# Products of probabilities and values for two head groups back to back, with three sets of transposed probabilities

## What is computed

```python
x = x + mamba(layernorm(x))            # a state-space mixer with a residual of its own
x = x + xattn(layernorm(x), ctx, mask) # 16 heads of 16 features over 512 x 512 scores
x = x + ffn(layernorm(x))              # each position goes through one of 8 matrices

# xattn, for each batch, head and query:
scores = Q @ K.T / 4 + adj; scores[mask == 0] = -inf
out = softmax(scores) @ V              # then the output projection
```

## Time and profile before

| | us |
|---|---|
| median of 3 runs | 1271.53 |
| lowest and highest | 1267.21, 1273.34 |
| the profiled execution: its time | 1269.45 |
| its span, first to last instruction | 1267.7 |

### The profile page before, as it was taken

How to read it: one execution, slowest core, us unless ns; L and a number is a source line. 1 busy time by engine, 2 the same in 40 slices (tenths; PEclk the granted TensorE clock), 3 DMA queues, 4 the chain that set the end, 5 groups by cost and what they waited for, 6 DMA issues and landing times. The chain is left out here.

```text
span 1267.7 us, 29908 instructions
## 1 busy us (share of the span) xinstructions
PE 1141.1 (90%) x10292; PEld 788.5 (62%) x10292; DVE 996.4 (79%) x2530; ACT 782.1 (62%) x1452; POOL 636.1 (50%) x554
## 2 busy tenths in 40 slices
PE   4587999999999999999999999999999999887387
PEld 2255666666667677666766666767776676655244
DVE  5765888788879887888888887888888887755486
ACT  2224675767776677667766766767566776766242
POOL 4572466327833584446544773278144653300375
PEclk9798999999999999999999999999899999989699
DMA  6042105410432024401540053103240143020511
GB/s 206 0 117 76 51 1 146 116 32 26 113 96 85 26 68 105 122 4 42 133 129 16 26 151 99 46 26 103 75 124 2 45 98 96 25 57 19 208 78 58
DMA packets 101524, 96.52 MB, mean 76 GB/s; under 512 B 17184, under 2 KB 76832, under 8 KB 100096
## 3 DMA queue, kind: packets, MB, share of 16 engines
q1 hardware_dynamic: 92912, 76.42, 20.0%
q0 software_dynamic: 6240, 17.57, 5.9%
q10 hardware_dynamic: 2224, 0.62, 0.2%
HBM read 71.49 MB, written 27.26 MB: 78 GB/s over the span
## 5 line engine op out<-in xcount | busy, mean ns | idle before, releaser
L902 ACT ACTIVATE T<-T,nmx 128x512 f32<-128x512 f32 x512 | 368.7, 723 | 215.6 <-DVE nmx L1269 213.6
L1269 DVE CUSTOM_DVE_ANT_0 T<-ps,am 128x512 f32<-128x512 f32 x512 | 346.3, 684 | 117.0 <-PE ps L687 115.2
L695 PE MATMUL pt<-ident,T 128*128 128x128 f32 x2048 | 324.8, 283 | 15.2 <-ACT PT L893 14.4
L695 PEld LDWEIGHTS pt<-ident,T 128*128 128x128 f32 x2048 | 231.9, 142 | 121.0 <-issue 87.8
L893 ACT COPY PT<-pt 128x512 f32<-128x512 f32 x352 | 201.9, 573 | 15.8 <-PE pt L695 15.1
L1385 POOL TENSOR_TENSOR dmask<-triu,dA 128x1024 fp32r<-128x1024 f32 x64 | 132.5, 2134 | 49.7 <-DVE dA L1113 49.5
L687 PE MATMUL ps<-k_st,q_st 64*128 64x512 f32 x512 | 131.0, 504 | 22.1 <-DMA q_st<-q_d 21.6
L712 PE MATMUL po<-PT,va 128*32 128x128 f32 x4096 | 139.2, 277 | 10.4 <-issue 6.2
L1360 POOL TENSOR_TENSOR xc<-xc,ygT 128x512 f32<-128x512 f32 x90 | 119.5, 1328 | 13.4
L1423 POOL TENSOR_TENSOR rr<-se,nhalf 128x1 f32<-128x1 f32 x32 | 22.1, 690 | 207.2 <-DVE se L1199 200.2
L712 PEld LDWEIGHTS po<-PT,va 128*32 128x32 f32 x4096 | 105.4, 110 | 33.3 <-issue 32.1
(11 more groups left out here) (216 smaller groups left out, 1950.3 us busy)
## 6 DMA issues: line engine op xcount, KB each, us to landing
k_st<-k_d SPq DMA_DIRECT2D x256, 64.0 KB, 2.2
q_st<-q_d SPq DMA_DIRECT2D x256, 64.0 KB, 2.4
am<-in_mask SPq DMA_DIRECT2D x8, 1024.0 KB, 5.4
k_d<-kp SPq DMA_DIRECT2D x32, 256.0 KB, 2.7
am<-in_adj POOLq DMA_DIRECT2D x8, 1024.0 KB, 10.6
q_d<-qp SPq DMA_DIRECT2D x128, 64.0 KB, 1.6
x_in<-in_x SPq DMA_DIRECT2D x8, 512.0 KB, 4.4
ctx_in<-in_ctxT SPq DMA_DIRECT2D x8, 512.0 KB, 4.1
```

The costliest lines, as they stand in the source:

```text
L695: ins = pe.transpose(pt[u % 2][:, kt * P:(kt + 1) * P], T[:, u % RING, kt * P:(kt + 1) * P], ident[:, :])
L902: act.activation(T[:, u % RING, :], T[:, u % RING, :], ACT.Exp, bias=nmx[:, u % RING:u % RING + 1], scale=-1.0).then_inc(sems["probs"], 1)
L1269: dve.tensor_tensor_reduce(T[:, u % RING, :], ps[(a * UNITS + u) % S_BANKS][:, :], ams[a % 2][:, qt, :], -1.0, 3e38, ALU.add, ALU.min, nmx ...
```

## The change

- **Pairs.** A product block is issued in every eighth unit's slot, for two groups one behind the other: groups n-1 and n (n odd) in slot 4n+7, where before only group n's stood. Group n-1 comes four slots later than it did.
- **Three sets.** `PT` has `SETS = 3` sets. They are used in turn over all batches, and `evac` of group n waits for the product of group n-3.
- **17 columns.** `va` holds 17 columns a head instead of 32: the 15 zeros are gone. Heads still start 32 columns apart in the array (`VT = 32`). The rows of `po` that no product writes any longer are cleared once at the start, on VectorE, and the first product waits for that.
- **Memory.** `x_in` and `ctx_in` become one tile `xio`; `st` lies on `th`; `b_f` lies on `pre` and the fourth row buffer on `xio`. The fetch of biases waits for the last convolutions instead of the products of batch 6.

```diff
-VW = 32
+VW = 17
+VT = 32
+SETS = 3
...
-        x_in = sb("x_in", [P, C, E])
-        ctx_in = sb("ctx_in", [P, KE, S])
-        st, mv, ve, rs = sb("st", [P, C, 6]), sb("mv", [P, C, 2]), sb("ve", [P, C, 2]), sb("rs", [P, C, 2])
+        xio = sb("xio", [P, 2, C * E])
+        x_in = xio[:, 0, :].rearrange("p (c e) -> p c e", c=C)
+        ctx_in = xio[:, 1, :].rearrange("p (k s) -> p k s", k=KE)
+        mv, ve, rs = sb("mv", [P, C, 2]), sb("ve", [P, C, 2]), sb("rs", [P, C, 2])
...
+        st = th[:, 1, 0:C * 6].rearrange("p (c n) -> p c n", n=6)
...
-        PT = sb("PT", [P, 2, HG, C, P])
+        PT = sb("PT", [P, SETS, HG, C, P])
...
-               xc[:, :, :].rearrange("p c s -> p (c s)")[:, 0:ROW], vas[1][:, :, :, :].rearrange("p c h v -> p (c h v)"),
+               xc[:, :, :].rearrange("p c s -> p (c s)")[:, 0:ROW], xio[:, :, :].rearrange("p i n -> p (i n)"),
...
-        b_f = vas[0][:, :, :, :].rearrange("p c h v -> p (c h v)")[:, 0:BLOCKS * E].rearrange("p (k e) -> p k e", e=E)
+        b_f = pre[:, :, :].rearrange("p n s -> p (n s)")[:, 0:BLOCKS * E].rearrange("p (k e) -> p k e", e=E)
...
                 def pv(a, n):
                     g = n % G
+                    if a == 0 and n == 0:
+                        pe.wait_ge(setup["sums"], 1)
...
-                            ins = pe.matmul(po[VW * hh:VW * (hh + 1), g * P:(g + 1) * P], vas[a % 2][:, kt, g * HG + hh, :], PT[:, n % 2, hh, kt, :],
-                                            start=(kt == 0), stop=(kt == C - 1), tile_position=(0, VW * hh), skip_group_check=True)
+                            ins = pe.matmul(po[VT * hh:VT * hh + VW, g * P:(g + 1) * P], vas[a % 2][:, kt, g * HG + hh, :], PT[:, (a * GROUPS + n) % SETS, hh, kt, :],
+                                            start=(kt == 0), stop=(kt == C - 1), tile_position=(0, VT * hh), skip_group_check=True)
...
-                    if 0 <= a < B and v % HG == 0:
+                    if 0 <= a < B and v % (2 * HG) == HG:
+                        pv(a, v // HG - 1)
                         pv(a, v // HG)
...
-                    act.wait_ge(sems["pv"], at("pv", a, n - 1))
-                    act.copy(PT[:, n % 2, v % HG, :, :].rearrange("p k i -> p (k i)"), pt[v % 2][:, :]).then_inc(sems["evac_act"], 1)
+                    act.wait_ge(sems["pv"], at("pv", a, n + 1 - SETS))
+                    act.copy(PT[:, (a * GROUPS + n) % SETS, v % HG, :, :].rearrange("p k i -> p (k i)"), pt[v % 2][:, :]).then_inc(sems["evac_act"], 1)
...
+                dve.memset(po[:, :], 0.0).then_inc(setup["sums"], 1)
...
-                pool.wait_ge(sems["pv"], at("pv", B - 1, 0))
+                pool.wait_ge(sems["conv_dve"], DC * sum(len(conv_split(b)[1]) for b in range(B)))
+                pool.wait_ge(sems["conv_pool"], DC * sum(len(conv_split(b)[0]) for b in range(B)))
```

More of the change, by code:

```diff
@@ L278, in build @@
         seg_expert = sb("seg_expert", [1, SEGS], I32)
-        flat = PT[:, :, :, :, :].rearrange("p o h k i -> p (o h k i)")
+        flat = PT[:, 0:2, :, :, :].rearrange("p o h k i -> p (o h k i)")
         rt = kp[:, :, :, :].rearrange("p o k s -> p (o k s)").bitcast(F32)[:, 528:528 + sum(RT.values())]
@@ L301, in build @@
         m_read = [sem(f"m_read{k}") for k in range(M_BANKS)]
-        setup = {n: sem(f"setup_{n}") for n in ("act", "dve", "pool", "scaled", "pad")}
+        setup = {n: sem(f"setup_{n}") for n in ("act", "dve", "pool", "scaled", "pad", "sums")}
         PER = dict(
@@ L1273, in evac @@
                     dve.wait_ge(sems["turned"], at("turned", a, v + 1))
-                    dve.wait_ge(sems["pv"], at("pv", a, n - 1))
-                    dve.tensor_copy(PT[:, n % 2, v % HG, :, :].rearrange("p k i -> p (k i)"), pt[v % 2][:, :]).then_inc(sems["evac_dve"], 1)
+                    dve.wait_ge(sems["pv"], at("pv", a, n + 1 - SETS))
+                    dve.tensor_copy(PT[:, (a * GROUPS + n) % SETS, v % HG, :, :].rearrange("p k i -> p (k i)"), pt[v % 2][:, :]).then_inc(sems["evac_dve"], 1)
                 def norm_heads(a, qt):
```

## The result

| | before | after |
|---|---|---|
| median of the runs, us | 1270.17 (6 runs) | 1289.29 (6 runs) |
| lowest and highest | 1265.11, 1273.34 | 1288.58, 1295.14 |
| profiled execution: time, span | 1269.45, 1267.7 | 1289.15, 1287.4 |

The ratio is 1.0165, with a 95% interval of 1.0135 to 1.0195: slower, where 1260 was forecast and 1249 to 1273 given.

The account below looks back on a forecast made before the run. TensorE's own instruction sequence was taken to set the pace from 116 to 1063 us. 11.4 + 0.8 + 3.5 - 2.4 - 1.9 = 11.4 us off the profiled 1269.45 gave 1258.1, as a median 1260; range 1249 to 1273.

Parts of the forecast that it names:

- "Pairing": TensorE's product blocks: issuing two in one visit removes the even block's own visit and saves 11.4 us of TensorE time.
- "1.21 becomes 0.11": Where a removed product had a full-size TensorE stage behind it, transposes to that stage shrink from 1.21 to 0.11 us.
- "What a pair delays": Copies of sums, transposes and scores behind a pair come later; one wait for probabilities in each of six batches, -2.4 us.
- "a queue that has 41 us free": ScalarE's queue per full batch: its free time was to absorb 3.5 us a batch of standing before copies of sums.
- "Edits with one answer ... all nothing": Bank clearing, smaller POOL clears, memory aliases and the bias gathers' new wait: no time; clearing 0.7 us once if uncovered.
- "Weights of 17 columns": TensorE's weight loads for products: the first load of each of 64 visits is 13 ns shorter, saving 0.8 us.
- the third set: PT evacuations wait for the product three groups back; their waits were to stay at nothing, 0 us.
- "Narrow loads pay in full": Rival: each of 4096 product weight loads gets 13 ns shorter, 52 us in all, giving 1210 us; chance 0.04.
- "Waits in front of products": TensorE stood 10.4 us before products in the whole run; a third, 3.5 us, counted as saved.
- "Scores starved": Rival: both products between two score pairs make VectorE run dry, up to 0.87 us a pair, 1281 us with 24; chance 0.09.
- "Absorbed": Rival: TensorE's saving turns into waits on chains of other engines and DMAs, 1266 to 1272, say 1269 us; chance 0.25.

Follow-up runs that it names:

- e10: Changed kernel with VectorE's split of the queries of a batch's first tile two slots earlier (slot 56 for 58): 1275.03 us, ratio 1.0047 to the kernel before.
- e9: Kernel before with VectorE's split of the queries of a batch's first tile two slots earlier (slot 56 for 58): 1255.20 us, ratio 0.9894.
- e13: e10 with GpSimd's last-chunk convolution (batches 1 to 7) and its sum of x and normed x cut to 8 columns: 1260.12 us, ratio 0.9931.
- e11: e8 (memory part and bank clearing alone) with the query split two slots earlier: 1260.78 us, ratio 0.9923 to the kernel before.
- e12: Changed kernel with GpSimd's last-chunk convolution (batches 1 to 7) and sum of x and normed x cut to 8 columns: 1276.07 us, ratio 1.0061.
- e1: Changed kernel with products issued one group at a time in the old slots; three sets, 17 columns and shared memory stay: 1279.04 us, ratio 1.0064.
- e8: Changed kernel reduced to its memory part and bank clearing: one product per slot, two sets, 32 columns: 1277.79 us, ratio 1.0062 to the kernel before.
- e5: Changed kernel with each pair split into separate visits, the even group's product in slot 4n+10, the odd one's in 4n+7: 1296.58 us, ratio 1.0212.
- e3: Changed kernel with GpSimd's sum of x and normed x issued behind a mask transfer instead of ahead of it: 1304.91 us, ratio 1.0294.

## Why the prediction was wrong

- **"Pairing", 11.4 us: right as a price of instructions, wrong as time.** Steps of 0.11 us, no border inside, 64 visits: all as costed (its terms add up to 11.5). Of the 8.9 us that they put in batches 1 to 6, TensorE's busy time shows 3.8 (e10 against e9) to 7.2 (e13 against e11). The step that failed is "1.21 becomes 0.11" (or 0.20): it takes for granted that the stage behind a product taken away is ready. At several of those places it was not; the product had covered the end of the chain that makes it ready. e13 against e11 is the measure: under 1 us of 11.4 shows, and four waits that e11 does not have (zs, ygT, xnT, qf) take 10.3.
- **"What a pair delays", -2.4 us: wrong by the most.** The forecast looked at probabilities alone, which hardly got late, and bounded the rest by slack in the mean: "a queue that has 41 us free". Delays came through at two places instead, the first product on convolved x and the bank behind the gate product, some 10 to 13 us together (e12, less the 3.5 that e1 has too). A mean of free time says nothing about the one instruction that is late, or about which of two engines comes first.
- **"Edits with one answer ... all nothing": wrong by 8 us (e8).** The aliases add no instruction, but the query load lands some tenths later, TensorE's clock falls behind more of these waits, and in one batch GpSimd's sum comes ahead of the gate product. With the load out of the way 5.6 us stay (e11 against e9). The load was in the rows as 1.6 us a batch; the clock and the order of the two engines were not in the sum. Why the load lands later and why the order flips, whether by where the tiles lie in memory or otherwise, stays open; that was not tried.
- **"Weights of 17 columns" 0.8 and the third set 0: not against the runs.** e1 and e8, which differ in them, lie 1.2 us apart. "Narrow loads pay in full" falls: sets stay 0.109 us apart, though a load is recorded at 98 ns for 110.
- **"Waits in front of products", 3.5 us: not settled.** All 10.4 us are gone from that place, but new waits stand elsewhere, and the runs don't tell how much of the 10.4 came back in them.
- **The rivals.** "Scores starved" had the sign, at 0.09, but not the cause (e5). "Absorbed" named the mechanism that decided, waits on chains of other engines, and stopped it at zero. It had no reason to stop there: work that stands later than before can cost more than the saving.

The sum by the runs: some 9 us for the memory part and 10 for the pairs (e1 lies between them), which is the 19 lost. Within the pairs' 10, what TensorE's instructions save is eaten by the four waits, and the two junctions come on top. Their 13 us must not be added to the memory part's 8: a flip of 3.5 us is in both, and the parts come from different runs, with some 4 us of width each.

## What to carry to other kernels

In a program whose engines each follow a fixed order, ask for every block that is taken from a place what stands behind it there and when its inputs are ready; and for every block put in, which chain on another engine begins behind it. Batches with few waits are tuned to that order, not free of dependences. When the bound engine stands for a load at a border, as 1.6 us a batch here, look first at whether its chain can start earlier: one due time gave 1.1% (e9), about as much as the whole change was forecast to give.

## What the runs showed of the hardware

- Two instructions that meet on VectorE and GpSimd cost unequally by their order. In the kernel before, with the product's start 0.14 us ahead, it takes 0.72 us and GpSimd's sum 2.86 for 2.37. With the sum's start ahead by 0.21 to 0.73 us the product takes 2.7 to 2.2 and ends 0.55 us after the sum. In e3 it takes 3.5 although its start is 0.14 us ahead, so recorded starts so close don't tell the order. Beside a sum in four pieces it takes 1.25 us and ends 1.3 us before the last piece: it does not wait for the whole row of them.
- A wait of some 2 us can cost 1.1 us more behind it: after 1.60 us the granted clock stayed at 1.00, after 2.16 it was 0.60 over the next 4.28 us. Its length alone does not decide: after 2.02 us the clock stayed at 1.00, after 1.76 it fell, both in the kernel before.
